# Causal masks moved from TensorE to VectorE, and two far mixes from VectorE to ScalarE, in a hand-scheduled attention kernel

## The reference

```python
s_cmp = jnp.einsum('bhnd,bmhd->bhnm', q, k_cmp) * scale        # k_cmp: means over blocks of 64
p_cmp = softmax(where(cmp_mask, s_cmp, -1e30)) * cmp_mask.any(-1)
p_slc = softmax(where(slc_mask, s_full, -1e30))                # s_full = q k^T * scale, causal
p_swa = softmax(where(swa_mask, s_full, -1e30))                # causal, the last 64 positions
o = o_cmp * g_cmp + o_slc * g_slc + o_swa * g_swa              # gates
x = x + o.reshape(b, n, H * HD) @ Wo
```

## Time and profile before

| what | value |
|---|---|
| median of 3 runs | 2455.5 us (2453.14 to 2456.52) |
| the profiled execution | 2451.99 us |
| its span in the profile | 2450.2 us |
| TensorE busy | 2377.8 us, 97% |
| VectorE busy | 1885.4 us, 77% |
| GpSimd busy | 1590.6 us, 65% |
| ScalarE busy | 1365.9 us, 56% |
| mask matmuls (L644) | 512, 51.1 us busy |

### The profile page before, as it was taken

The page is one execution under the profiler, slowest core; times in us unless marked ns, Lnnn a source line. Parts: engine busy times, 40 slices in busy tenths (PEclk is TensorE's granted clock), DMA queues, the critical chain, the costliest instruction groups (busy, mean ns, idle before and its releaser), DMA issues. The chain is left out here.

```text
span 2450.2 us, 43156 instructions
## 1 busy us (share of the span) xinstructions
PE 2377.8 (97%) x13968; PEld 2095.1 (86%) x13968; DVE 1885.4 (77%) x5847; ACT 1365.9 (56%) x3680; POOL 1590.6 (65%) x1206
## 2 busy tenths in 40 slices
PE   6899999999999999999999999999969999999998
PEld 5799989999998989999899989999967888887776
DVE  7488888888888888888888888888873777776224
ACT  7466666666666667666666666666653222213442
POOL 1677877787787778778777777787743333343342
PEclk9999999999999999999999999999979999999999
DMA  5212222222222222213221322222226323432366
GB/s 168 72 53 66 71 74 55 71 72 65 61 76 70 57 65 80 66 53 84 61 66 52 93 55 63 70 67 61 57 74 218 120 103 137 151 107 78 103 185 219
DMA packets 143214, 215.47 MB, mean 88 GB/s; under 512 B 15137, under 2 KB 53409, under 8 KB 141985
## 3 DMA queue, kind: packets, MB, share of 16 engines
q1 hardware_dynamic: 143008, 212.95, 29.3%
HBM read 94.66 MB, written 51.12 MB: 59 GB/s over the span
## 5 line engine op out<-in xcount | busy, mean ns | idle before, releaser
L553 POOL TENSOR_TENSOR s_full<-s_full,rope 128x512 f32<-128x512 f32 x256 | 335.5, 1311 | 352.3 <-DMA s_swap<-s_full 351.7
L557 POOL TENSOR_TENSOR s_full<-s_full,s_swap 128x512 f32<-128x512 f32 x256 | 331.4, 1294 | 36.7
L813 DVE TENSOR_REDUCE shift<-bank 128x1 f32<-128x512 f32 (+3 forms) x512 | 247.5, 483 | 113.1 <-PE bank L644 113.1
L561 POOL TENSOR_TENSOR qk_lo<-s_full,qk_hi 128x512 fp32r<-128x512 f32 x256 | 328.3, 1296 | 7.5 <-ACT qk_hi L712 5.0
L554 POOL TENSOR_TENSOR s_swap<-s_swap,rope 128x512 f32<-128x512 f32 x256 | 330.9, 1292 | 0.0
L717 ACT ACTIVATE pt_hi<-bank 128x384 fp32r<-128x384 f32 (+1 forms) x384 | 174.7, 528 | 261.4 <-PE bank L656 261.2
L997 POOL TENSOR_TENSOR o_lo<-o_raw,o_hi 128x2048 fp32r<-128x2048 f32 x32 | 149.7, 4678 | 241.6 <-ACT o_hi L1111 202.0
L611 PE MATMUL bank<-wv_hi,xt_hi 128*128 128x256 f32 x1024 | 299.5, 292 | 0.0
L723 ACT ACTIVATE bank<-bank,shift 128x512 f32<-128x512 f32 (+3 forms) x512 | 256.3, 501 | 64.5 <-DVE bank L817 64.4
L611 PE MATMUL bank<-wv_hi,xt_lo 128*128 128x256 f32 x1024 | 290.2, 283 | 0.0
L611 PE MATMUL bank<-wv_lo,xt_hi 128*128 128x256 f32 x1024 | 289.6, 283 | 0.0
(11 more groups left out here) (183 smaller groups left out, 6971.6 us busy)
## 6 DMA issues: line engine op xcount, KB each, us to landing
s_swap<-s_full SPq DMA_DIRECT2D x512, 128.0 KB, 2.3
o_scratch<-s_swap SPq DMA_DIRECT2D x128, 256.0 KB, 2.0
o_raw<-o_scratch SPq DMA_DIRECT2D x32, 1024.0 KB, 6.0
w_raw<-in_L_ffn_W SPq DMA_DIRECT2D x64, 256.0 KB, 3.3
xin<-in_L_attn_x SPq DMA_DIRECT2D x14, 1024.0 KB, 5.5
base_scratch<-x SPq DMA_DIRECT2D x8, 1024.0 KB, 4.7
base<-base_scratch SPq DMA_DIRECT2D x32, 256.0 KB, 4.2
out<-base SPq DMA_DIRECT2D x32, 256.0 KB, 3.1
```

Of the source, the lines that this page charges most:

```text
L553: nc.gpsimd.tensor_tensor(s_full[k][:], s_full[k][:], rope[:, 0, :], ALU.mult).then_inc(cos_done[k], 1)
L557: nc.gpsimd.tensor_tensor(s_full[k][:], s_full[k][:], s_swap[k][:], ALU.add).then_inc(roped[k], 1)
L561: nc.gpsimd.tensor_tensor(qk_lo[k][:], s_full[k][:], f32(qk_hi[k][:]), ALU.subtract).then_inc(lo_done[k], 1)
L813: nc.vector.tensor_reduce(shift1[:, t:t + 1], n[:, 0:(t + 1) * P], AX.X, ALU.min)
```

## The change

The mask becomes an fp32 tile, loaded straight by DMA (it was loaded into `probs` and cast). VectorE adds it to each diagonal block in PSUM (`mask`, a new function): tiles 3 and 0 before it reads tile 3, tiles 2 and 1 after `pt_low`, before it reads tiles 2, 1 and 0. `scores_ready` now counts each tile's last score matmul, and `read` waits on a new semaphore, `causal_masked`. The far blocks of tiles 2 and 1 are scaled by ScalarE, one activation for each 64 columns (three and one), behind `evacuate` q and ahead of `values_high` of the next body; VectorE waits on `far_mixed` before it scales the near blocks of these tiles, and TensorE before the transposes. The near mix of tile 1 now stands ahead of the window mix of tile 2.

```diff
@@ attend
-    ident_h = r("ident_h", [P, P], BF16)
-    causal_h = r("causal_h", [P, P], BF16)
+    causal = r("causal", [P, P])
...
+    MASKED_AT = {3: 1, 0: 2, 2: 3, 1: 4}
+    FAR_AT = {2: 1, 1: 2}
@@ tensor, body
-                            nc.tensor.matmul(banks[t][:, 0:w], x[:, t * P:(t + 1) * P], v[:, 0:w], start=(n == 0), stop=(n == 2),
-                                             skip_group_check=True)
-                    for t in SCORED:
-                        nc.tensor.matmul(banks[t][:, t * P:(t + 1) * P], ident_h[:], causal_h[:], start=False, stop=True,
-                                         skip_group_check=True).then_inc(scores_ready, 1)
+                            last = nc.tensor.matmul(banks[t][:, 0:w], x[:, t * P:(t + 1) * P], v[:, 0:w], start=(n == 0), stop=(n == 2),
+                                                    skip_group_check=True)
+                        last.then_inc(scores_ready, 1)
...
+                    pe.wait_ge(far_mixed, (u - 2) * 2 + 2)
@@ scalar
+            def mix_far(v, t):
+
+                act.wait_ge(cmp_step, v * NC + 7)
+                for b in range(near(t)[1] // BS):
+                    last = nc.scalar.activation(probs[:, E1OFF[t] + b * BS:E1OFF[t] + (b + 1) * BS], banks[t][:, b * BS:(b + 1) * BS],
+                                                ACT.Identity, scale=coef[:, 1, t:t + 1], bias=cb[:, t, b:b + 1])
+                last.then_inc(far_mixed, 1)
@@ scalar, body, behind evacuate(u, 0)
+                if end:
+                    mix_far(u - 2, 2)
+                    mix_far(u - 2, 1)
@@ vector
-                dve.wait_ge(scores_ready, v * T + scored_at[t])
+                dve.wait_ge(causal_masked, v * T + MASKED_AT[t])
...
+            def mask(v, t):
+                block = banks[t][:, t * P:(t + 1) * P]
+                dve.wait_ge(scores_ready, v * T + scored_at[t])
+                nc.vector.tensor_tensor(block, block, causal[:], ALU.add).then_inc(causal_masked, 1)
@@ vector, body
-                    dve.wait_ge(scores_ready, v * T + scored_at[0])
+                    mask(v, 3)
+                    mask(v, 0)
                     read(v, 3)
                 if end:
                     for g in range(3):
                         pt_low(u, g)
                 if score:
+                    mask(v, 2)
+                    mask(v, 1)
                     for t in (2, 1, 0):
                         read(v, t)
...
                     mix_window(v, 0)
-                    mix_far(2)
                     mix_window(v, 3)
+                    dve.wait_ge(far_mixed, v * 2 + FAR_AT[2])
                     mix_near(2)
-                    mix_far(1)
+                    dve.wait_ge(far_mixed, v * 2 + FAR_AT[1])
+                    mix_near(1)
                     mix_window(v, 2)
-                    mix_near(1)
                     mix_window(v, 1)
```

More of the change, by code:

```diff
@@ L423, in attend @@
     out_ready, out_evacuated, out_slot_free, zeros_set = S("out_ready"), S("out_evacuated"), S("out_slot_free"), S("zeros_set")
+    causal_masked, far_mixed = S("causal_masked"), S("far_mixed")
     gates_squashed, gates_stored, gates_loaded = S("gates_squashed"), S("gates_stored"), S("gates_loaded")
@@ L519, in middle @@
                     quad(p, k)
-            sp.dma_start(probs[:, 0:P], misc_d[:, MISCW:MISCW + P]).then_inc(causal_loaded, 16)
+            sp.dma_start(causal[:], misc_d[:, MISCW:MISCW + P]).then_inc(causal_loaded, 16)
             sp.dma_start(rope[:].rearrange("p a n -> p (a n)"), rope_d).then_inc(rope_loaded, 16)
@@ L917, in quad @@
                 body(p, k, 3, split=split)
-            nc.vector.memset(sc, 0.0).then_inc(zeros_set, 1)
-            nc.vector.tensor_copy(ident_h[:], m("ident")).then_inc(zeros_set, 1)
+            nc.vector.memset(sc, 0.0).then_inc(zeros_set, 3)
             dve.wait_ge(causal_loaded, 16)
-            nc.vector.tensor_copy(causal_h[:], probs[:, 0:P]).then_inc(zeros_set, 1)
             gc = gates_full[:, :, 0, :]
```

## The result

| | before | with the change |
|---|---|---|
| median of 4 runs, us | 2455.99 (2453.14 to 2456.52) | 2435.54 (2433.43 to 2442.18) |
| ratio, 95% interval | 1 | 0.9922 (0.9909 to 0.9934) |
| profiled execution, us | 2451.99 | 2433.43 |
| its span, us | 2450.2 | 2431.6 |
| VectorE busy, us | 1885.4 | 1913.1 |

Faster by 20.5 us or 0.8%, inside the range of 2421 to 2442 and 7.5 us short of the 2428 forecast. In the profiled executions the gain is 18.6 us against the 27.3 of the sum. The result has two sides: a unit became shorter by a little more than forecast, and part of that was given back in a few units.

The account below looks back on a forecast made before the run. TensorE's full instruction stream was taken as the bound; -29.4 + 2 + 0.1 = -27.3 us took the profiled 2452.0 to 2424.7, so 2428 from the median of 2455.5. The range was 2421 to 2442.

Parts of the forecast that it names:

- the sum: Forecast change of the profiled execution: -29.4 for the mask matmuls, +2 for late units, +0.1 at the end: -27.3 us.
- TensorE's term: Attention stage: four mask matmuls leave TensorE in each of 128 units, 0.23 us a unit, 29.4 us in all.
- VectorE's ring: Everything VectorE must do or sit through in an attention unit: 12.50 us before, 12.95 forecast, against TensorE's 13.28.
- the slack of 1.01 us: VectorE's wait for the mask matmuls before reading row tile 3, subtracted from the 13.51 us period to give 12.50.
- The far wait: VectorE's new wait for ScalarE's far mix before the near mix of tile 2, forecast at about 0.1 us.
- The step of 0.13 us: VectorE's wait for its own result between tile 1's near and window mixes, forecast to vanish in the new order.
- rival 1: VectorE becomes the bound in the attention units: period 13.4 us, a gain of 14 us, 2441 (2433 to 2448); chance 0.12.
- ScalarE's form: Price of a 64-column far activation with pointers for scale and bias: 0.41 us long, one each 0.30 us.
- What costs something back: VectorE's weight splits in 14 units make TensorE wait some 0.3 us in each pair, 2 us in all (0 to 8).
- seven pairs: The 14 attention units in which VectorE also splits weights, two in a row; 2.3 us of splits a pair.
- The margin of 1.34 us: How far window tile 0's end precedes the next scores that wait for it, forecast to absorb VectorE's lateness.
- tail: After the last projection the last far mix starts late, hidden by VectorE's blocked wo_lo: 0.1 us (0 to 1.8).
- Rival 2: Far mix on ScalarE arrives late at VectorE's near tile 2: wait 0.83 us, +22 us, 2477; chance 0.08.

Follow-up runs that it names:

- mixing locally: The changed kernel, but in the units in which weights are split VectorE mixes the far blocks of tiles 2 and 1 itself, in the old order: 2431.89 us.

## Why the prediction was right, and where it fell short

**TensorE's term: right.** -29.4 us was forecast, 125 periods shorter by 0.247 give -30.9. The four masks took 0.25 us: from the last score matmul to the transposes it was 0.36 us and is 0.12, and the 0.23 read from the first mask on left out a hundredth before it.

**VectorE's ring: right by errors that cancel.** Forecast 12.95 us; 13.02 by the waits of the trace, 12.9 where VectorE is behind and nothing but ScalarE holds it. The start, 12.50, was 0.08 us too long, because the slack of 1.01 us was counted from the end of `v_lo`, where the next instruction can start 0.08 us earlier. The masks cost 0.20 each instead of 0.25 (-0.2). The far wait costs 0.30 from start to start (0.21 shown as idle) instead of 0.1. The step of 0.13 us that was to go did go (the two near mixes and the two window mixes now stand close together). Masks at their whole duration (rival 1) are refuted by the 0.20.

**ScalarE's form: right.** 0.41 us long and 0.29 apart, forecast 0.41 and 0.30, from rows of other forms. The estimate by the Trainium skill's page (ScalarE: Activation LUTs, What ACT_TABLE_LOAD costs), 0.33 apart, is a little too high here, where the source lies in PSUM; its 93 ns a pointer fits the 185 ns for two of the earlier trace rows.

**The step that failed is "What costs something back".** It put 0.3 us on each of seven pairs, 2 us in all; they cost 0.9 to 1.0 each, 7.0 us. I counted VectorE's 0.6 and 1.1 us and left out that ScalarE's splits, 1.05 + 0.62 us, now stand ahead of something VectorE waits for. Moving 0.52 us of it away took 0.4 us off the stall, mixing locally took about the same off. VectorE's own share was sized too high in its length (0.68 in all 14 units of the changed kernel, where before every second took 1.6) and too low in its effect. The margin of 1.34 us was read at tile 0; TensorE stops at tile 2, and there it is 0.90. And the added work of the run with the split done twice went through to the time in full, once the margin was used up.

**What the sum left out** is the excess outside the pairs, 3.5 us more than before, and the first period's 0.8. In these units VectorE waits 0.9 to 1.7 us for ScalarE's exponentials instead of 0.71, and in most of them another 1.0 us for the far mix; TensorE stops 0.05 to 0.12 us for the probabilities, and in three of them 0.2 to 0.7 us before its scores (once for GpSimd's low parts, twice with no cause named). In the unit that I looked at more closely (at 578.7 us) it begins with a swap transfer that lands 1.5 us late, so that GpSimd's rotation and ScalarE's `high` q are late too. Waits of 1.3 to 2.0 us for the exponentials are in the trace of before as well, in four units, where the longer period absorbed most of it. That the shorter period is what exposes them is argued from the two traces; no run isolates it. The 2.2 us behind the last projection are all in the later stages, which the change doesn't touch.

Against the 27.3 us of the sum, 8.7 are missing: the pairs 5.0, other units and the first period 4.3, the end 2.1; the masks and the earlier start gave 2.7 more than forecast.

**The range.** 2422 to 2433 was called the sum's own bounds, but its terms (pairs 0 to 8, tail 0 to 1.8) give 2426 to 2436. The measured 2435.5 lies in that, and in the 2433 to 2448 that was meant for rival 1. Rival 1 is not what happened: TensorE is still the bound.

**The tail: right**, and for the reason given. From the last q projection to the first matmul of the output projection it was 47.60 us and is 47.42, with one set of masks (0.25) gone, so 0.07 us came back. The far mix came 2.57 us late there and the transposes started later, but the split that blocked VectorE was 4.02 us long instead of 6.03 and ended when it would have. VectorE, timeline at the stage's end:

```profile
1803.72 0.75 DVE L847 SCALAR_TENSOR_TENSOR bank<-bank,coef,cb 128x192 f32<-128x192 f32 x2 [2.57 <-ACT probs L743]
1805.03 4.02 DVE L1010 TENSOR_TENSOR wo_lo<-o_raw,wo_hi 128x2048 fp32r<-128x2048 f32 x1
```

GpSimd's instruction beside it starts at 1802.39 and lasts 4.51, to 1806.90; VectorE's ends 2.15 us behind it, as in the earlier trace rows.

**Rival 2**, the far mix arriving late, was refuted for the steady unit, and is what happened in seven units of 128. The run with tile 2's activations doubled shows what I had left out of it: at a wait of 0.88 us the period was 13.50, that of before (the rival's arithmetic gives 12.85 + 0.88 = 13.73), but the kernel was 49 us slower than before, all of it through the late units.

One claim was in none of the rivals: that the second half of the change was needed at all. The masks alone give 2435.7 us, the same within the intervals.

## What to carry to other kernels

When work moves off a full engine, the gain is its distance to the next instruction, times the repetitions; that part can be read to a few hundredths. What is given back comes from the irregular repetitions, so read those one by one, on every engine in the loop, and put the new wait behind whatever its producer does there once in a while. Two moves made together should be run apart: here one carried the whole gain and the other was worth nothing in the steady unit, since VectorE was not the bound without it either. And read an engine's spare time from start to start, in a unit in which it has to catch up; idle time counted from the end of an instruction leaves out what the overlap hides, here 0.08 us at each wait.

## What the runs showed of the hardware that I had not expected

- A 128x512 fp32 subtraction on VectorE with all operands in SBUF and one of GpSimd's instructions of that kind go one after the other. There are 196 such subtractions in the thirteen traces. The 89 that started with GpSimd idle lasted 0.68 us, even where GpSimd started a moment later. An instruction of GpSimd's that starts during one of them lasts up to 1.8 us in place of 1.29, and ends 1.13 to 1.33 us behind VectorE's. Of the 107 that started while GpSimd's was running, 105 ended 0.54 to 0.60 us behind it, and lasted up to 1.80; the other two started within 0.01 us of GpSimd's and lasted 0.68. So a shift of 0.6 us could turn 0.68 into 1.77. The masks, the mixes and `pt_lo`, which read PSUM, kept their durations beside GpSimd (the masks 0.29 us, with and without it).
- A VectorE add of a 128x128 block in PSUM with a block in SBUF lasts 0.29 us and costs 0.20 us in a row of two, less than the 0.25 us of the mixing instruction of that size, which takes a scalar from a pointer as well.
- The medians of the kernel before lie within 2455.2 to 2456.6 us on the chips used, those of the changed kernel at 2435.5 on one and 2439.9 on another. Single runs spread as much with either: 2450 to 2460 us before, 2433 to 2442 with the change. Whether the change lost some steadiness can't be told from these.
